# First attention: experts' down projection transposed over 512 tokens, gates spread by transfers, scores first in a chunk

## The chip, the cores and the metric

The kernel runs on one core of a Trainium2 chip. The time is that of the device for one launch, in microseconds (us); the kernel before takes 3878.38 us, the median of three runs (3876.18 to 3879.57). The core has TensorE (PE in the rows; its weight loads are PEld), VectorE (DVE), ScalarE (ACT), GpSimd (POOL) and SyncE (SP), which issues the transfers. Each runs its own list of instructions in order and waits for the others by semaphores. TensorE writes to PSUM only, which is eight banks of 128 x 512 float32.

## What is computed

16 sequences of 1024 tokens with 256 features go through two layers; all is float32. The first layer, cut to what matters:

```
xn = layernorm(x)
q, k, v = xn Wq, xn Wk, xn Wv                      # 16 heads of 16
g = log_sigmoid(xn Wgk1 Wgk2 + bgk2) / 16          # decay of each key feature
state = state * exp(g) + v k^T ; out = state q     # token by token
s = (layernorm(out) * gamma + beta) * silu(xn Wg) @ Wout
gates = softmax of the 2 largest of xn @ w_gate    # 8 experts, others 0
h = relu(xn @ Wd[e] + bd[e])                       # 8 experts of 64
f = sum over e of gates[e] * 0.5 * (h[e] @ Wu[e] + bu[e])
x = x + s * silu(f)
```

The second layer is a windowed attention with softmax and a ternary ffn of 1024 hidden features, joined in the same way.

## The kernel before

The body of the loop holds eight sequences one after another and is run twice. Of a sequence (NC = 8 chunks of 128 tokens) the parts are: queries and keys of the first attention for 512 tokens at a time (L1366 to L1383), the loop over chunks (from L1460), the second attention, and the ffn, in which the next sequence's norm, its routing logits, its decay inputs `z` and its first queries are made already.

In a chunk `c` TensorE goes in this order. `token_major(bank 0, c, w_vg)` makes values and output gate (512 columns, two steps over the 256 features, four records); two turns of the keys; `parity_scores` (L1432, the scores of 16 heads on 32-row parts of the array, into banks 3 to 6); `token_major(bank 2, c, w_down)`, the experts' down projection, tokens on the partitions; `cumulate(c + 1)` (L1384), the sums of the decays for the next chunk; then, with the masked scores, the output block: for each half of the features one product with the state (L1490) and 16 with the scores (L1495); four turns of `hg` (L1502); `output_turn(c - 1)` (L1411), the turn of the previous chunk's gated output; the state update (L1511); `output_project(c - 1)` (L1424); the up projection of four products of 256 columns (L1520) with the bias through the turned gates (L1526); and `attention_token_major(c)` (L1418), the turn of the output back to token rows.

VectorE in a chunk: values times decay (`vt`, L1160), output gate (`silu_g`, L1166), four masked scores (`causal_scores`, L1139), the gated output of the previous chunk (`y_tok`, L1105), bias add `hb` (L1175) and ReLU with the gates `hg` (L1179), state sum and state (L1187, L1191), `finish_chunk(c - 1)` (L1121 to L1129: gate product, residual, statistics), scaled output `o_tok` and its statistics (L1204 to L1209), `f_gate` (L1211), the next middle state (L1150), and `o_norm` (L1112). In chunk 7 six normalisations of the finished x (L1132) stand after `hg`. GpSimd makes the root of the variance, the two affine steps (L730, L734), `end_mask` (L765) and `parity_queries` for the next chunk (`qx`, L714). ScalarE makes tanh, the copies out of PSUM (`hgt`, L878, is that of the turned `hg`) and the three decays of a chunk (`decays`, L825 to L834), after a load of its function table at the first. At the end of the loop the normalised x is turned in eight steps (`chunk_turn`), four of them inside chunk 7's up projection, and the second attention begins with `queries_keys`. SyncE has one queue: loads of x, loads of the next sequence, stores.

The order on each engine is written out by hand as it stands in the code. The waits are counts of semaphores.

## Time and profile before

| what | value |
|---|---|
| median of three runs | 3878.38 us |
| profiled execution: own time, span | 3877.76 us, 3876.0 us |
| TensorE busy (its matmuls) | 3650.6 us, 94% |
| VectorE, ScalarE, GpSimd busy | 2777.5 us, 1962.9 us, 1082.2 us |
| GpSimd 128x512 products `qx` of the chunks (L714) | 136.4 us, 128 of them |
| VectorE `hb` (L1175), `hg` (L1179) | 86.9 us, 88.6 us |
| TensorE turns of `hg` (L1502) | 84.0 us, 512 of them |
| granted clock of TensorE | 0.996 |
| transfers | 62.3 MB, on average 16 GB/s |

A busy time of TensorE is no measure of how much is left there: records of matmuls overlap, so the distance from the start of one step to the start of the next is what a step costs. An idle time of an engine stands in brackets behind a row, with what ended it. All times in the rows below are from the start of the span; they are from the fifth sequence, and the other sequences go alike.

### The profile page before, as it was taken

How to read it: one execution, taken by the hardware profiler on the slowest of the kernel's cores; microseconds unless marked ns; L12 is line 12 of the kernel's file. 1: busy time of each engine (PE TensorE's matmuls, PEld its weight loads, DVE VectorE, ACT ScalarE, POOL GpSimd, SP SyncE). 2: the span in 40 equal slices, each digit the busy share in tenths (PEclk: the TensorE clock that was granted, in tenths of full speed). 3: DMA queues.
4: the chain of work that ended last, by engine and by line, in shares of the span. 5: the costliest groups of instructions: out<-in, count | busy, mean ns of one | idle time of the engine just before them, and what ended most of it. 6: DMA issues, size and time to landing. Idle time of an engine off the chain costs nothing. (4 is left out here: it accounts for less than half of the span.)

```text
span 3876.0 us, 73403 instructions
## 1 busy us (share of the span) xinstructions
PE 3650.6 (94%) x26748; PEld 2384.1 (62%) x26748; DVE 2777.5 (72%) x6223; ACT 1962.9 (51%) x4311; POOL 1082.2 (28%) x1313
## 2 busy tenths in 40 slices
PE   3999999999999999999989999999999999999999
PEld 2666566665666656566655666656666566665656
DVE  4767777777667767677666776777767766777767
ACT  2264562745536365373644726446274553636536
POOL 2323233231322313223122232323323232231322
PEclk9999999999999999999999999999999999999999
DMA  3000010000000000000000100001000010000000
GB/s 85 1 12 23 1 34 1 13 21 8 27 1 18 17 12 23 1 30 5 12 23 1 33 2 12 23 1 34 1 14 21 2 33 1 16 19 12 23 1 23
DMA packets 72652, 62.28 MB, mean 16 GB/s; under 512 B 18032, under 2 KB 71904, under 8 KB 72288
## 3 DMA queue, kind: packets, MB, share of 16 engines
q1 hardware_dynamic: 72288, 57.52, 4.9%
q8 instruction: 217, 3.56, 0.4%
q14 instruction: 147, 1.20, 0.1%
HBM read 40.72 MB, written 16.78 MB: 15 GB/s over the span
## 5 line engine op out<-in xcount | busy, mean ns | idle before, releaser
L786 POOL TENSOR_TENSOR qx<-qx 128x512 f32<-128x512 f32 x256 | 281.1, 1102 | 760.6 <-ACT qx L1003 760.6
L1251 DVE TENSOR_REDUCE row_max<-bank 128x4 f32<-128x512 f32 x512 | 339.2, 684 | 137.6 <-PE bank L1585 134.4
L1139 DVE TENSOR_TENSOR am<-bank,causal 128x512 f32<-128x512 f32 x512 | 317.2, 682 | 17.5 <-PE bank L1443 17.5
L1329 DVE TENSOR_TENSOR sq_lo<-qx,sq_hi 128x512 fp32r<-128x512 f32 x256 | 205.5, 803 | 155.0 <-ACT sq_hi L982 154.5
L1598 PE MATMUL bank<-ident,am 128*128 128x128 f32 x2048 | 297.1, 278 | 14.2 <-ACT qx L938 9.4
L1598 PEld LDWEIGHTS bank<-ident,am 128*128 128x128 f32 x2048 | 230.6, 141 | 92.1 <-issue 48.9
L1258 DVE TENSOR_TENSOR am<-bank,row_max 128x512 f32<-128x512 f32 x384 | 265.6, 692 | 14.6 <-PE bank L1598 1.1
L723 POOL TENSOR_SCALAR o_veps<-o_mom 128x1 f32<-128x1 f32 x128 | 28.5, 223 | 881.6 <-DVE o_mom L1209 879.3
L922 ACT ACTIVATE am<-am 128x512 f32<-128x512 f32 x384 | 261.1, 680 | 5.5 <-DVE am L1258 5.5
L1363 PE MATMUL bank<-w_down,xt 128*128 128x512 f32 x512 | 252.2, 615 | 0.0
L1520 PE MATMUL bank<-w_up,hgt 128*128 128x256 f32 x1024 | 246.2, 381 | 3.7 <-ACT hgt L878 3.7
L1363 PE MATMUL bank<-w_vg,xt 128*128 128x512 f32 x512 | 240.9, 593 | 0.0
L1693 PE MATMUL bank<-sq_hi,pj_t 128*128 128x512 f32 x512 | 213.7, 417 | 17.3 <-DVE sq_lo L1329 10.2
L825 ACT ACTIVATE decay_in<-bank 128x256 f32<-128x256 f32 x128 | 49.2, 384 | 340.8 <-PE bank L1396 340.6
L1520 PEld LDWEIGHTS bank<-w_up,hgt 128*128 128x128 f32 x1024 | 192.0, 190 | 31.5 <-ACT hgt L878 6.7
L780 POOL TENSOR_TENSOR xl<-xt,xh 128x1024 fp32r<-128x1024 f32 x32 | 75.5, 2359 | 457.1 <-DVE xh L1300 457.1
L1693 PE MATMUL bank<-sq_lo,pj_t 128*128 128x512 f32 x512 | 201.7, 394 | 0.0
L1003 ACT ACTIVATE qx<-bank,scale_fc 128x512 f32<-128x512 f32 x256 | 177.5, 693 | 43.5 <-PE bank L1681 43.5
L885 ACT ACTIVATE tanh_f<-bank 128x256 f32<-128x256 f32 x128 | 49.2, 384 | 289.6 <-PE bank L1526 289.6
L982 ACT CAST sq_hi<-qx 128x512 fp32r<-128x512 f32 x256 | 158.9, 621 | 68.4 <-PE bank L1693 37.0
L1187 DVE TENSOR_TENSOR state_sum<-bank,state_mid 128x256 f32<-128x256 f32 x112 | 47.6, 425 | 196.1 <-PE bank L1511 196.1
L714 POOL TENSOR_TENSOR qx<-qt,par_mask 128x512 f32<-128x512 f32 x128 | 136.4, 1066 | 176.6 <-ACT qt L436 138.3
(252 smaller groups left out, 8933.0 us busy)
## 6 DMA issues: line engine op xcount, KB each, us to landing
qt<-in_L_attn_x SPq DMA_DIRECT2D x136, 128.0 KB, 2.2
x<-in_L_attn_x SPq DMA_DIRECT2D x128, 128.0 KB, 2.3
out<-x SPq DMA_DIRECT2D x128, 128.0 KB, 1.7
x<-in_L_ffn_w_fc SPq DMA_DIRECT2D x1, 1024.0 KB, 5.7
attn<-in_L_ffn_w_proj SPq DMA_DIRECT2D x1, 1024.0 KB, 7.7
w_up<-in_L_ffn_Wu SPq DMA_DIRECT2D x1, 512.0 KB, 6.0
w_down<-in_L_ffn_Wd SPq DMA_DIRECT2D x2, 256.0 KB, 3.7
w_vg<-in_L_attn_Wv SPq DMA_DIRECT2D x1, 256.0 KB, 4.4
```

Source lines behind the costliest of these rows:

```text
L786: nc.gpsimd.tensor_tensor(sq[:, n % 3, :], relu[:, n % 3, :], relu[:, n % 3, :], ALU.mult)\
L922: nc.scalar.activation(pr[:, j], pr[:, j], ACT.Exp).then_inc(s["pr_ok"], 1)
L982: nc.scalar.copy(sq_hi[:, n % 3, :], sq[:, n % 3, :]).then_inc(s["sqh_ok"], 1)
L1003: nc.scalar.activation(relu[:, n % 3, :], bank[1 + n % 3][:], ACT.Relu, scale=scale_fc[:, n % MT:n % MT + 1]).then_inc(s["relu_ok"], 1)
L1139: nc.vector.tensor_tensor(am_tiles[:, :, j], bank[3 + j][:].rearrange("p (f e t) -> p f e t", f=2, e=2), causal[:].unsqueeze(1).unsqueeze( ...
L1251: nc.vector.tensor_reduce(row_max[:, j, :], scored, AX.X, ALU.max, negate=(j == 0))\
L1258: nc.vector.tensor_tensor(pr[:, j], scored, row_max[:, j, :].unsqueeze(2).broadcast_to([P, 4, P]), ALU.subtract).then_inc(s["sub_ok"], 1)
L1329: nc.vector.tensor_tensor(sq_lo[:, n % 3, :], sq[:, n % 3, :], sq_hi[:, n % 3, :].bitcast(F32), ALU.subtract)\
L1363: mm = nc.tensor.matmul(dst, xt[:, k, c * P:(c + 1) * P], w[:, k, :], start=(k == 0), stop=(k == KD - 1))
L1520: nc.tensor.matmul(bank[5][:, 0:D], hgt[:, j, :], w_up[:, j, :], start=(j == 0), stop=False)
L1598: mm = nc.tensor.transpose(bank[5 + n % 2][:, h * P:(h + 1) * P], pr[:, j, h, :], ident[:])
L1693: mm = nc.tensor.matmul(bank[5 + o][:], pj_t[:, m, o * P:(o + 1) * P], part[:, n % 3, :], start=(m == 0 and part is sq_hi), stop=(m == MT ...
```

## The change

- **Down projection.** `experts_down(i)` makes 128 of the 512 hidden features for 512 tokens, transposed: weights `w_down` as the stationary operand, `xt` as the moving one. Four groups (tokens 0 to 511, banks 0 to 3) stand before the loop between the queries and keys; the other four stand at the end of chunks 0 to 3, each into bank 5. ScalarE applies bias and ReLU (`experts_relu`) into `hidden_t`. `hb`, `hg`, `hgt` and their turns are gone.
- **Gates.** The gates stand in the turned gates once more as full float32 (32 rows further); ScalarE copies these rows, SyncE writes them to DRAM and reads each back to 64 partitions (two transfers of 512 KB for 512 tokens, into `g_wide`), and GpSimd multiplies the hidden features of a chunk with them (`hidden_gated`, 128x512, in place). The second 512 tokens' transfers wait for the product of chunk 3.
- **Order in a chunk.** The scores come first, then values, turn of keys, the up projection (into bank 2), the cumulative sums, the output block, in which both state products now stand ahead of all score products. Scores of chunks 1 to 4 wait for the last ReLU. On VectorE the values' product stands between the third and fourth masked scores.
- **End of the loop.** Two pairs of normalisations move to the ends of chunks 5 and 6 and their turns into chunk 7, in pairs. The query projection 1 moves ahead of the last output turn.
- Smaller: the gate turns stand before the last two keys; `u_nat`, `u_lo`, `w_kv2` share the space of `am`; the bias of the down projection is loaded once, not spread.

```diff
+    gate_banks = (1, 0)
+    up_banks = (2, 2, 2, 2, 2, 2, 2, 5)
# SyncE
+                    for g in range(NG):
+                        sp.wait_ge(s["gx_ok"], at("gx_ok", g + 1))
+                        sp.dma_start(gate_dram[g], gate_rows[8:8 + E, g * 512:(g + 1) * 512]).then_inc(s["gw_ok"], 16)
+                        sp.wait_ge(s["gw_ok"], at("gw_ok", 16 * (g + 1)))
+                        if g:
+                            sp.wait_ge(s["hm_ok"], at("hm_ok", 4))
+                        for e in range(2):
+                            rows = gate_dram[g].rearrange("(j e) t -> e j t", e=2)[e]
+                            sp.dma_start(g_wide[e * BN:(e + 1) * BN], rows.partition_broadcast(BN)).then_inc(s["gl_ok"], 16)
# GpSimd: hidden_gated(0) before the loop, hidden_gated(c + 1) after parity_queries(c + 1)
+                    def hidden_gated(c):
+                        g, cols = c // 4, slice(c % 4 * P, (c % 4 + 1) * P)
+                        pool.wait_ge(s["hr_ok"], at("hr_ok", 4 * (g + 1)))
+                        pool.wait_ge(s["gl_ok"], at("gl_ok", 32 * (g + 1)))
+                        nc.gpsimd.tensor_tensor(hidden_t[g][:, :, cols], hidden_t[g][:, :, cols], g_wide[:, :, cols], ALU.mult)\
+                          .then_inc(s["hm_ok"], 1)
+                        if c == NC - 3:
+                            rstd2(0, 0, 4)
# ScalarE, before decays(0)
+                    experts_relu(0)
+                    experts_relu(1)
+                    first_queries_keys(4)
+                    first_queries_keys(5)
+                    experts_relu(2)
+                    experts_relu(3)
+                    for b in range(NG):
+                        act.wait_ge(s["gtp_ok"], at("gtp_ok", b + 1))
+                        nc.scalar.copy(gate_rows[:, b * 512:(b + 1) * 512], bank[gate_banks[b]][32:64, :]).then_inc(s["gx_ok"], 1)
+                    for b in range(NG):
+                        nc.scalar.copy(gates_t[:, 4 * b:4 * b + 4, :], bank[gate_banks[b]][:].rearrange("p (c t) -> p c t", t=P))\
+                          .then_inc(s["gt_ok"], 1)
+                    first_queries_keys(6)
+                    first_queries_keys(7)
# VectorE, in a chunk
+                        for j in range(3):
                             causal_scores(c, j)
+                        dve.wait_ge(s["tg_ok"], at("tg_ok", c + 1))
+                        decayed_values(c)
+                        causal_scores(c, 3)
+                        output_gate(c)
                         if c:
                             gated_output(c - 1)
-                        nc.vector.tensor_add(hb[:], bank[2][:], bc_down[:]).then_inc(s["hb_ok"], 1)
-                        nc.vector.scalar_tensor_tensor(
-                            hg[:].rearrange("p (e b) -> p e b", e=E), hb[:].rearrange("p (e b) -> p e b", e=E), 0.0,
-                            g_all[:, c, :].unsqueeze(2).broadcast_to([P, E, BN]), ALU.max, ALU.mult)\
...
+                        if c in (NC - 3, NC - 2):
+                            dve.wait_ge(s["rs2"], at("rs2", 1))
+                            for b in range(2):
+                                normalise2(2 * (c - NC + 3) + b)
# TensorE, before the loop
+                    first_queries_keys(2)
+                    first_queries_keys(3)
+                    experts_down(0)
+                    experts_down(1)
+                    first_queries_keys(4)
+                    first_queries_keys(5)
+                    experts_down(2)
+                    experts_down(3)
+                    pe.wait_ge(s["gates_ok"], at("gates_ok", 7))
...
+                    first_queries_keys(6)
+                    first_queries_keys(7)
...
+                        elif c <= 4:
+                            pe.wait_ge(s["hr_ok"], at("hr_ok", 4 + c))
# TensorE, in a chunk
                     for c in range(NC):
+                        parity_scores(c)
...
+                            experts_up(c, 0)
+                            experts_up(c, 1)
                             cumulate(c + 1)
+                        else:
+                            pe.wait_ge(s["f1_ok"], at("f1_ok", c))
+                            pair_turn(0)
+                            pe.wait_ge(s["ktok_ok"], at("ktok_ok", c))
+                            pe.wait_ge(s["f2_ok"], at("f2_ok", c - 1))
+                            pair_turn(1)
...
-                        pe.wait_ge(s["hg_ok"], at("hg_ok", c + 1))
-                        for j in range(EB // P):
-                            mm = nc.tensor.transpose(bank[2][:, j * P:(j + 1) * P], hg[:, j * P:(j + 1) * P], ident[:])
...
+                        if c < 4:
+                            experts_down(4 + c)
+                        attention_token_major(c)
+                    experts_up(NC - 1, 1)
```

## Rows read from the trace of the kernel before

**Rows 1.** Busy time by stretch (start:end, us, busy by engine and instructions, clock, DMA).

```profile
1064.85:1127.21 62.36, 61.63 (x467) 41.18 (x465) 46.34 (x106) 17.06 (x45) 20.22 (x30) 1.00 0.01 2
...
1027.00:1262.80 235.80, 226.28 (x1667) 147.75 (x1667) 171.33 (x384) 121.75 (x269) 66.15 (x78) 1.00 0.05 15
```

**Rows 2.** Timeline of TensorE in a steady chunk: start, us, engine, line, operation.

```profile
1064.85 0.26 PEld L1422 LDWEIGHTS bank<-ident,ot 128*128 128x128 f32 x2
...
1065.08 0.30 PEld L1363 LDWEIGHTS bank<-w_vg,xt 128*128 128x128 f32 x2
...
1067.22 0.74 PEld L1443 LDWEIGHTS bank<-qx,k 32*128 32x128 f32 x16 [0.17 <-issue]
...
1068.29 0.30 PEld L1363 LDWEIGHTS bank<-w_down,xt 128*128 128x128 f32 x2 [0.33 <-issue]
...
1070.00 0.19 PEld L1395 LDWEIGHTS bank<-xh,cumulator 128*128 128x128 f32 x1 [0.55 <-issue]
...
1071.13 0.30 PEld L1490 LDWEIGHTS bank<-qt,state_mid 128*128 128x128 f32 x2 [0.34 <-DVE am L1139]
...
1071.55 0.38 PEld L1495 LDWEIGHTS bank<-am,vt 128*32 128x32 f32 x16
...
1073.12 0.42 PEld L1502 LDWEIGHTS bank<-ident,hg 128*128 128x128 f32 x4 [0.20 <-DVE hg L1179]
...
1073.74 0.20 PEld L1415 LDWEIGHTS bank<-ident,y_tok 128*128 128x128 f32 x2 [0.20 <-issue]
...
1074.64 0.51 PEld L1428 LDWEIGHTS bank<-w_out,yt 128*128 128x128 f32 x3 [0.20 <-ACT yt L841]
```

**Rows 3.** Timeline of VectorE and GpSimd in the same chunk.

```profile
1062.21 0.42 DVE L1187 TENSOR_TENSOR state_sum<-bank,state_mid 128x256 f32<-128x256 f32 x1 [1.76 <-PE bank L1511]
...
1065.39 0.42 DVE L1204 TENSOR_TENSOR o_tok<-bank,decay_out 128x256 f32<-128x256 f32 x1 [0.51 <-PE bank L1422]
...
1068.27 0.41 DVE L1166 SCALAR_TENSOR_TENSOR silu_g<-tanh_g,bank 128x256 f32<-128x256 f32 x1
...
1068.60 2.48 DVE L1139 TENSOR_TENSOR am<-bank,causal 128x512 f32<-128x512 f32 x4
...
1070.28 1.04 POOL L714 TENSOR_TENSOR qx<-qt,par_mask 128x512 f32<-128x512 f32 x1
...
1070.99 0.61 DVE L1105 TENSOR_TENSOR y_tok<-o_bet,silu_g 128x256 f32<-128x256 f32 x1
...
1074.66 0.42 DVE L1187 TENSOR_TENSOR state_sum<-bank,state_mid 128x256 f32<-128x256 f32 x1 [1.74 <-PE bank L1511]
```

**Rows 4.** Timeline, from the start of the loop over chunks to chunk 1's output block.

```profile
1036.61 1.65 POOL L738 TENSOR_TENSOR xl<-attn,xh 128x512 fp32r<-128x512 f32 x1 [7.01 <-DVE xh L1097]
...
1038.55 1.28 ACT L825 ACT_TABLE_LOAD   x1
...
1040.38 0.60 ACT L834 ACTIVATE decay_state<-bank 128x512 f32<-128x512 f32 x1
...
1058.64 0.49 PE L1490 MATMUL bank<-qt,state_mid 128*128 128x128 f32 x2
```

**Rows 5.** The page, section 5: a ReLU of 128x512 from PSUM on ScalarE.

```profile
L1003 ACT ACTIVATE qx<-bank,scale_fc 128x512 f32<-128x512 f32 x256 | 177.5, 693 | 43.5 <-PE bank L1681 43.5
```

**Rows 6.** The DMA issues: destination, source, queue, count, size, us to landing.

```profile
x<-in_L_ffn_w_fc SPq DMA_DIRECT2D x1, 1024.0 KB, 5.7
attn<-in_L_ffn_w_proj SPq DMA_DIRECT2D x1, 1024.0 KB, 7.7
...
b_q<-in_L_attn_bq SPq DMA_DIRECT2D x8, 0.1 KB, 1.6
```

**Rows 7.** Timeline of chunk 7 and the start of the second attention.

```profile
1133.47 0.49 PE L1490 MATMUL bank<-qt,state_mid 128*128 128x128 f32 x2 [1.05 <-DVE am L1139]
...
1135.00 2.02 DVE L1132 TENSOR_SCALAR xn<-x,moments,rstd 128x256 f32<-128x256 f32 x6
...
1147.34 0.41 PEld L1545 LDWEIGHTS bank<-xt,w_k2r 128*128 128x128 f32 x2
```

More of the change, by code:

```diff
@@ L850, in _ @@
                     decays(0)
-                    for b in range(2):
-                        act.wait_ge(s["gtp_ok"], at("gtp_ok", b + 1))
-                        nc.scalar.copy(gates_t[:, 4 * b:4 * b + 4, :], bank[gate_banks[b]][:].rearrange("p (c t) -> p c t", t=P))\
-                          .then_inc(s["gt_ok"], 1)
                     for c in range(NC):
@@ L1193, in _ @@
                         else:
[L1195 to L1196 removed]
+                            dve.wait_ge(s["rs2"], at("rs2", 2))
+                            for b in range(4, NC - 2):
                                 normalise2(b)
@@ L1399, in _ @@
                     cumulate(0)
-                    pe.wait_ge(s["gates_ok"], at("gates_ok", 6))
-                    for b in range(2):
-                        if b:
-                            pe.wait_ge(s["qk_ok"], at("qk_ok", 6))
-                        for j in range(4):
-                            mm = nc.tensor.transpose(bank[gate_banks[b]][:, j * P:(j + 1) * P], gates[:, 4 * b + j, :], ident[:])
-                        mm.then_inc(s["gtp_ok"], 1)
-                    token_major(bank[0][:], 0, w_vg).then_inc(s["vg_ok"], 1)
-                    token_major(bank[2][:], 0, w_down).then_inc(s["hp_ok"], 1)
                     def output_turn(c):
@@ L1490, in _ @@
                             nc.tensor.matmul(bank[7][:, half * P:(half + 1) * P], state_mid[:, half, :],
-                                             qt[:, half, c * P:(c + 1) * P], start=True, stop=False,
+                                             qt[:, half, c * P:(c + 1) * P], start=(half == 0), stop=False,
                                              skip_group_check=True)
+                        for half in range(2):
                             for e in range(2):
```

229 lines of the change are left out of this document (128 added, 101 removed).

## The prediction

> **What bounds the kernel now.** I read the busy time by stretch first, then one steady chunk of the first attention on TensorE, the same chunk on VectorE and GpSimd, then the start and the end of the loop over chunks, and last the transfers. One sequence takes 235.8 us; the first attention, from the first key projection at 1027.0, has 120 of them. In five steady chunks TensorE is busy 61.6 of 62.4 us, VectorE 46.3, GpSimd 20.2 [rows 1]. So a chunk (62.36 / 5 = 12.47 us) is bound by TensorE: its steps follow each other with little between them [rows 2]. VectorE has its longest wait ahead of the state sum, 1.7 us [rows 3]. The second attention and the ffn, the rest of the sequence, are not touched.
>
> The steps of a chunk, from the starts in [rows 2]: turn of the output to token rows 0.23, value and gate projection with the turn of the keys 2.14, scores 1.07, down projection 1.71, cumulative sums 1.13 with a 0.34 wait for VectorE (0.78 alone), output block 1.99, four turns of hg 0.62, then 0.90 to the output projection, and what is left of 12.47, 2.70, for output projection and up projection, by their records 0.76 and 1.94.
>
> **Work that goes from TensorE.** The turns of hg: 8 x 0.62 = 5.0 us in a sequence. The down projection stays as large: 8 groups of four records before and after, of 1.71 us each [rows 2]. Of the output block the two state products now stand together. In [rows 2] two such records take 0.42 where 128 columns twice need about 0.21 (a 512-column record takes 0.43, a quarter of 1.71), so about 0.2 goes at each change between 128x128 and 32-column products; one pair of changes goes, 0.39, bounded by 0 and 0.42. I take 0.39: the block is 1.60. On this the Trainium skill, "TensorEngine Tiling (Array Packing)", section "Tiling Modes", says that changing the tiling mode drains TensorE; it gives no price, and the 0.2 of the row stands.
>
> **Work that goes from VectorE, and what GpSimd gets.** hb and hg go, from y_tok to what is the state sum's wait now, which only shortens VectorE's lap. ScalarE gets eight ReLUs for eight copies of hgt, two copies of gate rows more and three turned-x copies fewer; its new cost is only where TensorE waits for it (below). GpSimd gets eight products of 128x512 in a sequence; parity's takes 1.04 and a contended one 1.65 [rows 3, 4]. GpSimd is idle for over half of a chunk, so their time is free, apart from what they block.
>
> **The start.** TensorE now does ten groups of 1.71 and eight turns (0.9, by four turns in 0.62 with a mode change in it) before the cumulative sums: 1027.0 + 18.0 = 1045.0. ScalarE copies the last keys (to 1045.7), then loads a table and makes three decays. In [rows 4] load and decays run from 1038.55 to 1040.98, 2.43 us, and hid behind gate turns, value and down projection. Now the scores come directly after the cumulative sums and wait for them: start 1048.2, a stall of 2.4. Scores and value projection and key turn end at 1051.4. Then the up projection waits for GpSimd's product, that for the gates' transfer. ScalarE has the gate rows at 1042.2 (down 3 ends at 1040.7, 0.2 latency, ReLU 0.69 [rows 5], and a copy of the same size, 0.6). The write to DRAM takes about 1.65 (nearest: a small transfer, 1.6), the spread of 1 MB 5.7 to 7.7 [rows 6], with 0.5 for the second issue: 1050.2 to 1052.2. I take 5.7, since its rows are long and the queue is empty then. The product 1.04 to 1.65: 1051.3 to 1053.9. So the stall is 0, with 2.5 as upper end. Up 1.94, cumulative sums 0.78, output block of chunk 0 at 1054.1, 1.60, state update 0.6 (of the 0.90), down projection 4 until 1058.05. On GpSimd the end mask and parity's product for chunk 1 are queued behind this product; both are short and wanted only after chunk 0's output block and at 1059. On ScalarE the gate's tanh now waits for the up projection ahead of the next decays, which start after the cumulative sums anyway.
>
> Here is a new wait: scores of chunks 1 to 4 wait for ScalarE's ReLU of the down projection issued just before (both use bank 5). Latency 0.2, ReLU 0.69 [rows 5], 0.05 back: 0.93, of which the turn of the output hides 0.23; everything of the next chunk is queued behind it on TensorE. So scores 1 start at 1059.0, and with 1.07 + 2.14 + 1.94 + 0.78 = 5.93 the output block of chunk 1 at 1064.9. Before it was at 1058.64 [rows 4]: 6.3 later, with 5.15 of down and 1.94 of up projection done earlier.
>
> **Chunks 1 to 7.** Output block to output block for 1 to 4: 1.60 + 0.90 + 0.76 + 1.71 + 0.93 + 5.93 = 11.83, against 12.47: 3 x 0.64 = 1.9 back. VectorE is ready in time there: scaled output to output block is 1065.39 to 1071.13 less the 0.33 of the gate, which now comes after the last scores = 5.41 [rows 2, 3], and it starts the scaled output 0.4 before the scores (0.54 after the turn, they 0.93), so it is ready 5.0 after the scores' start, and needed at 5.93. From chunk 5 on TensorE alone would need 9.4, but VectorE is now the bound: block to state sum 3.53 - 0.62 - 0.39 = 2.52; state sum to the next scaled output 2.67 ([rows 3] less its wait of 0.51), then 5.41: 10.6. GpSimd's new product stands right behind parity's, where y_tok wants to start, and y_tok already ends only 0.28 after parity's product ([rows 3], 0.61 us with it). That can hold output turn and state by 0.2 to 0.3: 10.8. Chunks 6 and 7 have two normalisations each in this lap, 0.7 (six in 2.02, [rows 7]): 11.5. So 1.7 + 1.0 + 1.0 = 3.7 back. At the output block of chunk 7 the new kernel is at 6.3 - 1.9 - 3.7 = 0.7 us behind.
>
> The Trainium skill, "SBUF — State Buffer", says that VectorE with two SBUF inputs and GpSimd lock each other out for a whole instruction. The y_tok row agrees. Taken to its worst it is the third rival below.
>
> **The end.** From chunk 7's output block to the key projection of the second attention 13.87 us [rows 7]. On the chain to the last y_tok go 0.62, 0.39 and about 0.3 (turns of x now stand earlier): 1.3. After it, query projection 1 (1.72) has moved ahead; in its place 0.7 of waiting for yt stays: 1.0. Together 2.3, bounds 1.0 and 2.7.
>
> **Sum.** 0.7 - 2.3 = -1.6 us in a sequence, 16 x 1.6 = 25. The profiled execution had 3877.8 (span 3876.0), 0.6 under the median: 3853. A smaller bias load and the move of small weights at the start are within 1 us; they stand behind w_down, last in the queue. SP's next entry, the next sequence's loads, comes long after the gates'. Second group of gates: asked for after the product of chunk 3, it has a whole lap of 11.8 for about 6.2, and costs nothing unless it takes twice that; GpSimd's next affine step is queued behind it.
>
> **Rivals.**
> A. The gates come late (slower): DRAM write, completion, 1 MB of reads and the product form one chain of 9.1 us that ends when TensorE arrives. It decides from 1.6 us later on; at its upper ends (7.7 and 1.65) it costs 2.5: 0.9 x 16 = +15, 3893; if the repeated read of eight rows takes 10 us, 4.3 x 16 - 25 = +44. For it: nothing hides it and the whole start waits in order. Against: a row of 1 MB at 5.7.
> B. VectorE's lap isn't the bound, because waits in it overlap more than I see: chunks 5 to 7 take 9.5 to 10.2, 3 to 4 us less in a sequence: 3800. Against it: its steps come in fixed order, and rows carry each.
> C. The lock: y_tok always waits for the whole product, also in chunks 1 to 4, and normalisations meet GpSimd: 0.75 x 3 and some more: 2 to 3 in a sequence, 3890. Against it: GpSimd's steps are over when the state's come.
> D. Gains and stalls cancel, since all terms above (2.4, 4 x 0.7, laps) are near the 8.1 that TensorE saves: within 0.2%.
>
> **How the numbers follow.** Less than 0.2% (7.8 us) can hardly be told from no change. Forecast near 3853: 0.47; A 0.2; B 0.12; C 0.08; D 0.13. Faster 0.47 + 0.12 = 0.59, same 0.13, slower 0.28. The range takes in A's first price, C and most of B: 3808 to 3900.
>
> **What would show it.** Start: a TensorE idle of 2.4 before scores 0 released by ScalarE's decay_state; the product of chunk 0 ending near 1051. Chunks 1 to 4: 11.8 apart, 0.7 idle before the scores, released by the ReLU. Chunks 5 to 7: 10.8 to 11.5, TensorE idle before the output block, VectorE hardly idle. No turns of hg; output block 1.6. Key projection of the second attention 1.6 earlier. I am wrong if the start stalls at the up projection, if chunk 5 takes over 11.5, or if the second attention and ffn change their length.

## The result and the profile after

The changed kernel is slower. Its median is 3984.18 us (3981.94 to 3988.03, four runs) beside 3877.43 us of the kernel before on the same chip (3876.18 to 3879.57, four runs): ratio 1.0276, 95% interval 1.0258 to 1.0294. The forecast was 3853, its range ended at 3900. The profiled execution took 3983.88 us, its span is 3982.1 us (before 3876.0).

The page of the changed kernel, section 1 (busy us, share of the span, instructions):

```profile
PE 3577.9 (90%) x26236; PEld 2361.6 (59%) x26236; DVE 2637.5 (66%) x5983; ACT 2003.1 (50%) x4295; POOL 1265.4 (32%) x1473
```

And the view of the core, with its span and granted clock:

```profile
core 0: 3982.1 us, clock 0.980
```

TensorE's matmuls are busy for 72.7 us less than before (3650.6) and its share fell from 94% to 90%: the work went, and idle time came that is larger. The granted clock fell from 0.996 to 0.980. The trace of the granted clock shows TensorE at the lower of its two levels (1.2 instead of 2.4 GHz) for 163 us of the launch, and for 30 us before.

Next I measured stages, by the starts of the output blocks (ob) of chunks 0 to 7, the first product of a sequence's first key projection, and `w_k2r` of the second attention. Means over 14 sequences in us (the one at the loop's turn and the last are left out); "forecast" is worked out from the prediction's steps (its 13.87 us for the end counted to the weight load of `w_k2r`; to the first product it is 14.08, so the forecast stands here as 14.08 less 2.3):

| stage | before | forecast | after | at 1.2 GHz, after |
|---|---|---|---|---|
| first key projection to ob 0 | 20.31 | 27.1 | 28.88 | 2.79 |
| ob 0 to 1 | 11.42 | 10.8 | 10.51 | 0 |
| ob 1 to 4, three laps | 37.43 | 35.5 | 37.35 | 0 |
| ob 4 to 5 | 12.47 | 10.8 | 11.17 | 0 |
| ob 5 to 6 | 12.47 | 11.5 | 12.33 | 0 |
| ob 6 to 7 | 12.47 | 11.5 | 13.06 | 2.58 |
| ob 7 to `w_k2r` | 14.08 | 11.8 | 14.18 | 4.00 |
| rest of the sequence | 115.47 | the same | 115.36 | 0 |
| sum | 236.1 | 234.5 | 242.8 | 9.4 |

So 6.7 us more in a sequence, 16 times: 107 us, the whole difference. The forecast is missed by 8.3 us in a sequence, in five places: the start (+1.8), the laps of chunks 1 to 4 (+1.9), the laps 4 to 6 (+0.4, +0.8), the lap to chunk 7 (+1.6) and the end (+2.4); the lap from 0 to 1 came out 0.3 shorter than forecast.

What TensorE waited for in the whole launch (line that waited, what it waited for, us in total, times, longest):

```profile
PE bank L1499 <- ACT ot L930: 65.2, 112, 0.6
PE bank L1592 <- DVE am L1191: 47.8, 48, 2.0
...
PE bank L1527 <- ACT attn L849: 41.7, 64, 0.7
PE bank L1527 <- ACT decay_state L881: 39.7, 16, 2.5
PE bank L1537 <- DVE xn L1184: 25.4, 16, 1.7
PE bank L1488 <- DVE am L1191: 24.1, 32, 1.4
...
PE bank L1555 <- POOL qx L769: 6.0, 6, 1.2
```

Third and fourth are the two waits of the forecast (0.65 before scores 1 to 4, 2.48 before scores 0). The first, 112 times 0.58 us, was not in it: the output turn waits for ScalarE's copy `ot`, because the turns of `hg` that stood between them are gone. TensorE before, in the chunk of [rows 2]:

```profile
1072.54 0.64 PE L1495 MATMUL bank<-am,vt 128*32 128x128 f32 x16
1073.12 0.66 PE L1502 MATMUL bank<-ident,hg 128*128 128x128 f32 x4
1073.77 0.41 PE L1415 MATMUL bank<-ident,y_tok 128*128 128x128 f32 x2
```

From the end of the output block (1073.18) to the output turn are 0.59 us here too, and the turns of `hg` fill them. Of the waits of the changed kernel, the second, fifth and sixth are VectorE's laps in chunks 5 to 7. The last is the transfer's, and it is only 6.0 us in 6 times. The kernel before waited 37 us for the masked scores in all.

TensorE's timeline of the start (fifth sequence; start us, us, line, names; the idle time before it and what ended it in brackets). It answers to [rows 4]:

```profile
1054.61 3.60 PE L1438 MATMUL bank<-xt,w_k 128*128 128x512 f32 x8
...
1076.00 1.73 PE L1527 MATMUL bank<-qx,k 32*128 32x256 f32 x16 [2.48 <-ACT decay_state L881]
1077.66 3.05 PE L1417 MATMUL bank<-w_vg,xt 128*128 128x512 f32 x4
...
1080.76 1.89 PE L1555 MATMUL bank<-w_up,qx 128*128 128x256 f32 x8
```

GpSimd in the same stretch, the product with the gates:

```profile
1078.97 1.27 POOL L769 TENSOR_TENSOR qx<-qx,g_wide 128x512 f32<-128x512 f32 x1 [7.43 <-DMA g_wide<-gate_rows]
```

Busy times by stretch of the changed kernel, one stretch behind each of three waits (us; PE, PEld, DVE, ACT, POOL; granted clock; DMA):

```profile
1076.00:1080.70 4.70, 4.70 (x22) 2.47 (x23) 2.31 (x4) 0.00 (x0) 1.73 (x2) 0.64 0.38 72
1155.00:1158.40 3.40, 2.82 (x38) 2.07 (x37) 0.65 (x1) 0.64 (x2) 0.37 (x1) 0.51 0.02 5
1168.00:1175.50 7.50, 6.81 (x48) 5.25 (x49) 1.39 (x6) 0.74 (x2) 0.00 (x0) 0.54 0.00 0
```

Behind the wait of 2.48 us the clock is 0.64 on average, and scores and value projection take 1.73 and 3.05 us instead of 1.15 and 1.98. The up projection starts at 1080.76, 0.5 us after GpSimd's product has ended (1080.24): in this sequence the late transfer is covered by a slow clock.

TensorE's timeline in chunk 2, a lap that was to be 11.83 us:

```profile
1100.61 1.15 PE L1527 MATMUL bank<-qx,k 32*128 32x256 f32 x16 [0.65 <-ACT attn L849]
1101.68 1.98 PE L1417 MATMUL bank<-w_vg,xt 128*128 128x512 f32 x4
...
1106.27 0.61 PE L1592 MATMUL bank<-qt,state_mid 128*128 128x128 f32 x4
1106.81 1.08 PE L1598 MATMUL bank<-am,vt 128*32 128x128 f32 x32
1108.47 0.41 PE L1499 MATMUL bank<-ident,y_tok 128*128 128x128 f32 x2 [0.58 <-ACT ot L930]
```

TensorE in chunks 6 and 7:

```profile
1153.14 0.35 PE L1488 MATMUL bank<-xh,cumulator 128*128 128x256 f32 x1 [1.26 <-DVE am L1191]
...
1154.58 0.92 PE L1592 MATMUL bank<-qt,state_mid 128*128 128x128 f32 x4 [0.50 <-DVE am L1191]
1155.43 1.94 PE L1598 MATMUL bank<-am,vt 128*32 128x128 f32 x32
...
1165.47 0.63 PE L1537 MATMUL bank<-ident,xn 128*128 128x128 f32 x4 [1.69 <-DVE xn L1184]
1168.10 0.81 PE L1592 MATMUL bank<-qt,state_mid 128*128 128x128 f32 x4 [2.00 <-DVE am L1191]
```

And VectorE in chunk 6, with the last pair of normalisations in chunk 7:

```profile
1150.66 1.14 DVE L1184 TENSOR_SCALAR xn<-x,moments,rstd 128x256 f32<-128x256 f32 x2
...
1154.78 0.87 DVE L1157 TENSOR_TENSOR y_tok<-o_bet,silu_g 128x256 f32<-128x256 f32 x1
...
1168.64 0.72 DVE L1184 TENSOR_SCALAR xn<-x,moments,rstd 128x256 f32<-128x256 f32 x2
```

In chunk 2 the output block is 1.62 us from its start to the end of its last product (1106.27 to 1107.89; before, counted the same way, 2.05: 1071.13 to 1073.18). The forecast's 1.60 and 1.99 of [rows 2] are counted from start to start, so they compare only roughly. The wait before the scores is 0.65 as forecast, and ahead of the output turn TensorE stands idle for 0.58. In chunk 6 TensorE waits 1.26 and 0.50 for VectorE's masked scores, in chunk 7 1.69 for the second pair of normalisations and 2.00 for the scores. Behind these waits the clock is 0.51 and 0.54: the 32 score products take 1.94 where they took 1.08. The two normalisations take 1.14 us beside GpSimd's affine step (`o_gam`, 1150.82 to 1151.65), and 0.72 at 1168.64, where no instruction of GpSimd runs; `y_tok` takes 0.87 beside the product with the gates.

### The profile page after: what moved, and what is told of

It is laid out like the page before. It is cut to its first block and busy times, and to the rows that moved or that the text cites. A ratio compares the mean times of both kernels' runs of the same rounds, so it can differ in the third digit from the quotient of the medians.

```text
span 3982.1 us, 72507 instructions
## 1 busy us (share of the span) xinstructions
PE 3577.9 (90%) x26236; PEld 2361.6 (59%) x26236; DVE 2637.5 (66%) x5983; ACT 2003.1 (50%) x4295; POOL 1265.4 (32%) x1473
## 5 line engine op out<-in xcount | busy, mean ns | idle before, releaser
L1191 DVE TENSOR_TENSOR am<-bank,causal 128x512 f32<-128x512 f32 x512 | 327.0, 679 | 14.6 <-PE bank L1527 14.6
L907 ACT ACTIVATE tanh_g<-bank 128x256 f32<-128x256 f32 x128 | 49.2, 384 | 492.9 <-PE bank L1417 492.9
L1417 PE MATMUL bank<-w_vg,xt 128*128 128x512 f32 x512 | 266.3, 645 | 0.0
L1458 PE MATMUL bank<-xt,w_down 128*128 128x512 f32 x512 | 235.4, 592 | 0.0
L1527 PE MATMUL bank<-qx,k 32*128 32x256 f32 x2048 | 151.2, 409 | 81.3 <-ACT attn L849 41.7
L989 ACT COPY xn<-bank 128x512 f32<-128x512 f32 x256 | 154.0, 608 | 55.5 <-PE bank L1690 52.4
L1768 PE MATMUL bank<-xh,fc_t 128*128 128x512 f32 x512 | 173.9, 420 | 0.0
```

The costliest lines, as they stand in the source:

```text
L1191: nc.vector.tensor_tensor(am_tiles[:, :, j], bank[3 + j][:].rearrange("p (f e t) -> p f e t", f=2, e=2), causal[:].unsqueeze(1).unsqueeze( ...
L1417: mm = nc.tensor.matmul(dst, xt[:, k, c * P:(c + 1) * P], w[:, k, :], start=(k == 0), stop=(k == KD - 1))
L1458: mm = nc.tensor.matmul(bank[5 if g else j][:], w_down[:, k, j * P:(j + 1) * P], xt[:, k, g * 512:(g + 1) * 512], start=(k == 0), stop=(k ...
L1527: mm = nc.tensor.matmul(bank[3 + j][:, half * 2 * P:(half + 1) * 2 * P], kt[rows, half, c * P:(c + 1) * P], qp[rows, c % 2, half], start=T ...
L1768: nc.tensor.matmul(h_bank, fc_t[:, k, m * P:(m + 1) * P], t[:, g, k, :], start=(t is xh and k == 0), stop=False)
```

## The experiments

All runs of one batch share the runs of the kernel before (medians 3875.4 to 3877.2). Edits are of the changed kernel if nothing else is said.

**e1, the clock: useless work in the gaps.**

```diff
                     for c in range(NC):
+                        if c == 0:
+                            fill(bank[2][:, 0:D], 5)
...
+                            fill(bank[1][:, D:2 * D], 3)
                             pair_turn(1)
+                            fill(bank[7][:, 0:D], 4)
```

`fill(dst, n)` makes `n` products of `w_out` with itself, 256 columns each, whose result nobody reads.

> The changed kernel with useless products of TensorE put where it now stands idle: 5 of 256 columns (0.43 us each) ahead of the scores of chunk 0, 3 and 4 in chunk 7 ahead of the second pair of turns and of the output block. No wait is taken away. Theory 1 (the new idle lets the granted clock fall, and the work behind it runs at half speed: 163 us at the lower level in the changed kernel against 30 before): the time at the lower level goes to below 60 us, laps 6 to 7 and the end of the loop become 0.8 and 1.9 us shorter, the start 0.3, in all some 3 us in a sequence: 3935 (3920 to 3950). Theory 2 (only the waits themselves cost; the clock is a side effect of no weight): no gain, 3984 or a little more.

Measured: 3956.34 us, ratio 1.0208 (1.0191 to 1.0225), 28 us less than the changed kernel with more work in it. Time at 1.2 GHz fell from 163 to 62 us. The end went from 14.18 to 12.57 us; the start only from 28.88 to 28.59. TensorE's timeline of the start in e1 says why:

```profile
1066.67 2.32 PE L1563 MATMUL bank<-w_out 128*128 128x256 f32 x10
1069.31 1.15 PE L1527 MATMUL bank<-qx,k 32*128 32x256 f32 x16 [0.32 <-issue]
...
1073.51 1.99 PE L1555 MATMUL bank<-w_up,qx 128*128 128x256 f32 x8 [0.92 <-POOL qx L769]
```

Scores 0 and the values run at full clock, and now TensorE is at the up projection 0.92 us before the gates. What the clock gives back in the start the transfer takes. At the end of the loop nothing stood behind. So the clock is a cause, worth at least 28 us, but not the 49 us that I had expected: the end gave 1.6 us in a sequence, the start 0.3, and in the lap to chunk 7 nothing was won (2.4 us at 1.2 GHz for 2.6, 13.07 us for 13.06), although the longest wait for the masked scores there fell from 2.0 to 0.5 us.

**e2, the waits: another order in the chunk.** State update, output turn, down projection, then the output projection:

```diff
                             mm.then_inc(s["ds_ok"], 1)
+                        if c:
+                            output_turn(c - 1)
+                        if c < 4:
+                            experts_down(4 + c)
                         if c:
                             output_project(c - 1)
-                        if c < 4:
-                            experts_down(4 + c)
```

> The changed kernel with the state update ahead of the output turn, the down projection between output turn and output projection in chunks 1 to 3, and the first half of the last up projection ahead of the output turn in chunk 7. Theory A (the output turn waits 0.58 for ScalarE's copy of the output block, which the turns of hg used to hide, and the scores wait 0.65 for the ReLU): laps 1 to 4 go from 12.45 to 11.2 each, the end of the loop is 0.6 shorter, laps 4 to 7 stay (bound by VectorE's chain through the output projection), 4.3 us in a sequence: 3984 - 69 = 3915. Theory B (these waits only move: something else is as late): laps stay near 12.4, 3975 to 3985.

Measured: 3985.12 us, 1.0281 (1.0264 to 1.0299). Both waits are gone from the three laps between chunks 1 and 4 (the ReLU's stays before scores 1, 0.65 us in 16 times), and nothing is won; the three laps took 12.12, 12.21 and 12.78 us instead of 12.45, 0.24 us less together, and the end 14.33 instead of 14.18. That is the expectation's theory B. VectorE ahead of chunk 2's masks in e2:

```profile
1100.82 0.42 DVE L1173 SCALAR_TENSOR_TENSOR sf<-f_gate,bank 128x256 f32<-128x256 f32 x1 [2.05 <-PE bank L1512]
```

TensorE in the same chunk of e2:

```profile
1106.28 0.36 PE L1488 MATMUL bank<-xh,cumulator 128*128 128x256 f32 x1 [0.22 <-DVE am L1191]
...
1107.71 0.71 PE L1592 MATMUL bank<-qt,state_mid 128*128 128x128 f32 x4 [0.49 <-DVE am L1191]
```

`sf` needs the output projection, which came later, and waits 2.05 us (0.26 in the changed kernel); so the masked scores come later, and TensorE waits for them. So VectorE's chain from the output projection to the masks was close behind TensorE. The lap to chunk 4 has one thing more, on VectorE in e2:

```profile
1125.72 1.00 DVE L1176 TENSOR_TENSOR x<-x,sf 128x256 f32<-128x256 f32 x1
```

GpSimd beside it:

```profile
1125.17 1.27 POOL L769 TENSOR_TENSOR attn<-attn,g_wide 128x512 f32<-128x512 f32 x1 [4.71 <-ACT attn L849]
```

The residual add, 0.42 us in other chunks, takes 1.00 while GpSimd multiplies chunk 4's hidden features, which wait for the last ReLU: 0.58 us, the difference between 12.78 and 12.2.

**e3 and e4, the transfer under another order.** In chunk 0 values and turn of the keys stand ahead of the scores; e4 also has no transfers, and its hidden features are multiplied by ones, so it leaves the gates out of the up projection's main part.

```diff
                     for c in range(NC):
-                        parity_scores(c)
                         if c:
+                            parity_scores(c)
...
                             mm.then_inc(s["kp_ok"], 1)
+                            if c == 0:
+                                parity_scores(0)
                             experts_up(c, 0)
```

> The changed kernel with values, output gate and turn of the keys ahead of the scores in chunk 0 alone, as before: 2.1 us of work under the wait for ScalarE's decays. Theory C (the gates' transfer stands just behind that wait: its product ends 0.5 us before TensorE comes): start to the first output block goes from 28.9 to 28.4 only, 3976. Theory D (the wait of 2.5 us and the fall of the clock after it are all that holds the start): 28.9 to 25.3, 3926.

> As the run before, and without the gates' transfers: the hidden features are multiplied by ones that are set once, so the gates are left out of the up projection's main part. Theory C: now the start goes to 25.3 (3.1 us less than with the transfers), 3926 to 3935. Theory D: the same as the run before.

Measured: e3 4006.75 us, 1.0336 (1.0315 to 1.0357), start 30.46 us; e4 3934.92 us, 1.0153 (1.0136 to 1.017), start 25.72. In e3 the values hide all but 0.54 us of the decays, and TensorE is at the up projection 22.5 us after the sequence's first key projection (1060.33) instead of 26.1. There it waits (its timeline in e3):

```profile
1081.72 1.15 PE L1527 MATMUL bank<-qx,k 32*128 32x256 f32 x16 [0.54 <-issue]
1085.98 3.68 PE L1555 MATMUL bank<-w_up,qx 128*128 128x256 f32 x8 [3.11 <-POOL qx L769]
```

3.11 us of waiting, and the up projection then takes 3.2 us until its last step instead of 1.54: what was a wait for ScalarE has become a longer wait for the transfer, with half the clock behind it. The pair gives the transfer's full price in this order, 4.7 us in a sequence. It is not its price in the changed kernel, which e8 measures.

**e5, the normalisations back at the end.** Undoes the moves to chunks 5 and 6; all six normalisations stand in chunk 7 again.

```diff
-                        if c in (NC - 3, NC - 2):
-                            dve.wait_ge(s["rs2"], at("rs2", 1))
-                            for b in range(2):
-                                normalise2(2 * (c - NC + 3) + b)
...
-                            for b in range(4, NC - 2):
+                            for b in range(NC - 2):
# TensorE: pair_turn(0) and pair_turn(1) behind attention_token_major(NC - 1)
```

> Undoes one part of the change: the six normalisations stand together in chunk 7 again and the first two pair turns stand behind the last output projection, as in the kernel before. Own theory (the move costs more in chunks 5 and 6 than it saves at the end): the steps from output block 5 to 6 and 6 to 7 fall from 12.33 and 13.06 us to about 11.2 each, as the step from 4 to 5 has it, and the stage from output block 7 to w_k2r grows from 14.18 us by 1 to 2 us, so -1 to -2 us in each of the 16 sequences: 3952 to 3968 us. Rival (the normalisations only change place, as VectorE has the same work): the end grows by the full 3.0 us, 3980 to 3990 us.

Measured: 3943.91 us, 1.0169 (1.0152 to 1.0186), 40 us less than the changed kernel, more than I had expected. The laps to chunks 6 and 7 fell to 11.28 and 11.38 us, and the end stayed at 14.07 (14.18); 0.8 of the 1.7 us won in the lap to chunk 7 goes with the time at 1.2 GHz, which fell there from 2.6 to 0.1 us. The start was 0.4 longer (29.32), with 4.5 us at 1.2 GHz instead of 2.8, in the same order of work. TensorE's output block of chunk 7 in e5:

```profile
1159.02 0.68 PE L1584 MATMUL bank<-qt,state_mid 128*128 128x128 f32 x4 [3.86 <-DVE am L1190]
```

VectorE's timeline in the same chunk:

```profile
1159.71 1.70 DVE L1183 TENSOR_SCALAR xn<-x,moments,rstd 128x256 f32<-128x256 f32 x5
1164.78 0.42 DVE L1172 SCALAR_TENSOR_TENSOR sf<-f_gate,bank 128x256 f32<-128x256 f32 x1 [3.37 <-PE bank L1507]
```

The normalisations stand where VectorE has 3.37 us of idle time behind them: there they cost nothing. Moved into laps that VectorE bounds, they cost their whole time and the clock besides.

**e6, one part of the change alone in the kernel before: the order in the output block.**

```diff
-                                             ... start=True, stop=False,
+                                             ... start=(half == 0), stop=False,
                                              skip_group_check=True)
+                        for half in range(2):
                             for e in range(2):
```

> The kernel before with one part of the change alone: in the output block the two state products stand together, ahead of the 32 products of 32 columns. It took 1.99 us per chunk before and 1.60 us in the changed kernel. Own theory (TensorE's instructions set the laps of before, and VectorE has about 1 us of slack in them): 8 times 0.39 us in each of 16 sequences, -50 us, so about 3826 us (3820 to 3835). Rival (VectorE or the copies of ScalarE are close behind and take the place): 3850 to 3876 us.

Measured: 3835.98 us, 0.9896 (0.9879 to 0.9912): faster than both kernels. A lap went from 12.47 to 12.15 us, 0.32 instead of 0.39. A wait for VectorE stands where the other 0.07 may be; its timeline in e6 has:

```profile
1060.59 0.69 DVE L1179 SCALAR_TENSOR_TENSOR hg<-hb,g_all 128x512 f32<-128x512 f32 x1
```

And TensorE in the same chunk of e6, output block and turns of `hg`:

```profile
1059.47 0.71 PE L1490 MATMUL bank<-qt,state_mid 128*128 128x128 f32 x4
...
1061.33 0.66 PE L1503 MATMUL bank<-ident,hg 128*128 128x128 f32 x4
```

`hg` ends at 1061.28 and its turns start at 1061.33, 0.13 after the output block (1061.20). From its start to that end the block takes 1.73 instead of 2.05, which is the 0.32. What the block would give without `hg` behind it was not measured.

**e7, cover for the copy `ot`.** The cumulative sums of the next chunk stand behind the output block; ScalarE makes the decays behind `ot` and `yt`.

```diff
                             experts_up(c, 1)
-                            cumulate(c + 1)
...
                         mm.then_inc(s["ot_ok"], 1)
+                        if c + 1 < NC:
+                            cumulate(c + 1)
                         if c:
                             output_turn(c - 1)
```

> The changed kernel with the 0.70 us of the next chunk's cumulated decays on TensorE moved from ahead of the output block to right behind it, and ScalarE's three decay activations behind its copies ot and yt. Own theory (the hidden activations' turns of before covered 0.58 us in which TensorE now waits for ScalarE's copy ot before the output's turns): the steps from output block 1 to 4 fall from 12.45 us to about 11.87, so 3 times 0.58 us in 16 sequences, -28 us, with up to 15 us more from the chunks behind: 3940 to 3957 us. Rival (the wait only moves, to the decays' products or to VectorE): 3975 to 3990 us.

Measured: 3958.3 us, 1.0216 (1.0199 to 1.0233), 26 us less than the changed kernel. The laps from 1 to 2 and 2 to 3 are 11.89 and 11.88 us (12.45), the forecast's 11.83 but for 0.05. The third, from 3 to 4, is 12.36: TensorE waits 0.32 us for the masks in chunk 4, since VectorE's `state_mid` ran beside GpSimd's product for chunk 4 (0.77 us for 0.42) and GpSimd's root for `o_norm` stands behind that product. TensorE's timeline of e7 in chunks 3 and 4:

```profile
1110.94 0.39 PE L1489 MATMUL bank<-xh,cumulator 128*128 128x256 f32 x1
...
1111.75 0.38 PE L1500 MATMUL bank<-ident,y_tok 128*128 128x128 f32 x2
...
1121.75 0.71 PE L1592 MATMUL bank<-qt,state_mid 128*128 128x128 f32 x4 [0.32 <-DVE am L1192]
```

VectorE in chunk 4's lap of e7:

```profile
1117.02 0.77 DVE L1203 TENSOR_TENSOR state_mid<-state,decay_state 128x256 f32<-128x256 f32 x1
```

The turn at 1111.75 has no idle time before it. So the 0.58 is ScalarE's copy, uncovered by the removal of the turns of `hg`. Of the 26 us about 20 come from these three laps. The start is 0.8 us shorter (28.08), because the sums for chunk 1 stand behind its output block now, and the laps 4 to 5 and 5 to 6 are 0.2 and 0.1 longer: from chunk 4 on the wait for the copy is gone and a longer one for the masked scores stands there (107 us for `am` in the launch instead of 72). Chunk 7, where no sums are left to move, keeps its 0.58.

**e8, the changed kernel without the transfers, and e12, the same with e1's useless products.** The diff of both takes out SyncE's loop over `g` and GpSimd's wait on `gl_ok`, and sets `g_wide` to ones; both leave the gates out of the up projection's main part.

> The changed kernel without the transfers that write the gate rows out and spread them over the partitions; the hidden activations are multiplied by ones, so the gates are left out of the down path. Order of the work as in the changed kernel. Own theory (with the scores first the transfer has 7 us of cover, and TensorE reaches the up projection at most 0.6 us after the product is there): the start to output block 0 goes from 28.88 to 28.0 to 28.9 us, total 3970 to 3984 us. Rival (the transfer is on the path as in the run with the values' product first, where taking it away gave 4.7 us in each sequence): start about 24.2 us, total about 3910 us.

> The first fill run (useless products ahead of scores 0, in chunk 7 and behind it) without the transfers that spread the gates; the hidden activations are multiplied by ones, so the gates are left out of the down path. In the changed kernel taking the transfers away gave nothing, but the one sequence without half clock in its start took 27.06 us there against 28.3 with the transfers. Theory (half clock and transfer hide each other, each worth 1 to 1.3 us): with the clock held, start to output block 0 falls from 28.25 to 27.1 us, total 3935 to 3942 us. Rival (the transfer costs nothing in either case): 3953 to 3960 us.

Measured: e8 3986.65 us, 1.0279 (1.0262 to 1.0296), no gain. e12 3928.91 us, 1.0132 (1.0116 to 1.0149), 27 us less than e1. Starts of single sequences tell it best, us:

| start of a sequence | with the transfers | without |
|---|---|---|
| part of it at 1.2 GHz, the most frequent value (changed kernel, e8) | 28.7 | 28.7 |
| none at 1.2 GHz (changed kernel five times, e8 once) | 28.2 to 28.5 | 27.06 |
| with useless products, none at 1.2 GHz (e1, e12) | 28.1 to 28.4 | 27.06 |

The two prices hide each other: 1.2 us of late gates and up to 1.6 us of half clock, and the start pays the larger. Either one taken away alone gives nearly nothing (e1: 0.3 us, e8: none). With both away it takes the 27.1 us of the forecast. Between the profiled spans of e1 and e12 are 30 us. The start gives 1.25 x 16 = 20, by the means 28.59 and 27.34; the rest lies in the lap to chunk 7, where the clock held in e12 (12.28 us for 13.07) and not in e1, with the same order of work in it. So of the 27 us between e1 and e12 only these 20 are the transfer's price.

**e9, a start without the wait.** On TensorE the four down projections follow keys 2 and 3, then the turns of the gates, queries and keys 4 and 5, the cumulative sums, 6 and 7.

```diff
                     experts_down(1)
-                    first_queries_keys(4)
-                    first_queries_keys(5)
                     experts_down(2)
                     experts_down(3)
... the turns of the gates
+                    first_queries_keys(4)
+                    first_queries_keys(5)
+                    cumulate(0)
                     first_queries_keys(6)
                     first_queries_keys(7)
-                    cumulate(0)
# ScalarE: gate rows ahead of ReLU 2 and 3, decays(0) ahead of the copies of 6 and 7
```

> The changed kernel with another order ahead of scores 0, on TensorE: keys 2 and 3, the four down projections, the gates' turns, keys and queries 4 and 5, the cumulated decays of chunk 0, then 6 and 7 (before: the cumulated decays last). ScalarE copies the gate rows ahead of ReLU 2 and 3, and makes the decays ahead of the copies of 6 and 7. Own theory (the 2.48 us in which scores 0 wait for decay_state, and the half granted clock that follows it, are what the start took beyond its work): no wait before scores 0, so start to output block 0 from 28.88 us to 24.7 to 26.7, total 3920 to 3950 us. Rival (the transfer of the gates or ScalarE ends last instead): start 27.5 to 28.9 us, total 3960 to 3984 us.

Measured: 3928.97 us, 1.0135 (1.0118 to 1.0152), 55 us less than the changed kernel, as expected. The start takes 25.61 us on average, 25.33 in most sequences. TensorE's timeline of the start in e9:

```profile
1055.84 3.60 PE L1438 MATMUL bank<-xt,w_k 128*128 128x512 f32 x8
1059.37 1.15 PE L1527 MATMUL bank<-qx,k 32*128 32x256 f32 x16
...
1062.48 1.91 PE L1555 MATMUL bank<-w_up,qx 128*128 128x256 f32 x8
```

The gates' product on GpSimd in e9:

```profile
1061.07 1.27 POOL L769 TENSOR_TENSOR qx<-qx,g_wide 128x512 f32<-128x512 f32 x1 [4.44 <-DMA g_wide<-gate_rows]
```

No idle time before scores 0, full clock, and the product of the gates ends at 1062.34, 0.14 us before it is wanted. The wait for the decays was a matter of the order: the load of the function table and the decays (2.4 us) have two projections of 1.7 us to hide behind, if the sums stand before them.

**e10 and e11, the repairs together.** e10 has the edits of e5, e7 and e9, and in chunk 7 the up projection ahead of the output block, where e5 waits 3.86 us; e11 adds three useless products there.

> Four edits of the changed kernel together: the start's order of e9; the cumulated decays behind the output block; the normalisations and pair turns back in chunk 7; and in chunk 7 the whole up projection (1.9 us) ahead of the output block, where TensorE waited 3.86 us for VectorE's masks. If the parts add up: 3984 - 40 (norms at the end) - 26 (cumulated decays) - 34 to 62 (start) - 15 to 30 (up projection) = 3826 to 3869 us. If they share one bound, VectorE's lap of 11.3 to 11.9 us: 3870 to 3900 us.

> e10 with three useless products of 128 x 256 (0.43 us each) in chunk 7 ahead of the output block, inside the wait for VectorE's masks. Clock theory (the half granted clock behind that wait costs 1.3 to 1.5 us in each sequence): 20 us faster than e10 if the clock still falls there. Rival (with the up projection in that place the wait is too short for the clock to fall): the same as e10 within 5 us.

Measured: e10 3852.28 us, 0.9939 (0.9922 to 0.9955); e11 3840.3 us, 0.9905 (0.9888 to 0.9921). TensorE at the output block of chunk 7 in e10:

```profile
1122.76 0.71 PE L1583 MATMUL bank<-qt,state_mid 128*128 128x128 f32 x4 [1.76 <-DVE am L1189]
```

e11, the useless products and the output block:

```profile
1121.78 1.46 PE L1557 MATMUL bank<-w_out 128*128 128x256 f32 x6
1123.70 0.71 PE L1590 MATMUL bank<-qt,state_mid 128*128 128x128 f32 x4 [0.47 <-DVE am L1189]
```

With 1.76 us of waiting at this place e10 still spends 2.93 us of an end at 1.2 GHz on average: none in the first eight sequences, some in seven of the last eight, with the same wait in all. With 0.47 e11 spends none, the end takes 12.43 us in every sequence (13.36 on average in e10), and the launch is 12 us shorter. The parts add up: 55.2 + 40.3 + 25.9 = 121.4 us for e9, e5 and e7 singly; e10 has 10.5 more, which is put down to its up projection but was not run alone; e11 12.0 more; together 143.9, from 3984.2 to 3840.3.

## Why the prediction was wrong, point by point

**The sum.** Of the 8.3 us missed in a sequence, 4.1 are the wait for ScalarE's copy `ot` (seven chunks of 0.58), which the prediction put at nothing; 2.4 are the half clock in the end (1.6, e1) and in the lap to chunk 7 (0.8, by the sequences without it); 1.8 are the start, where late gates and half clock hide each other; 0.9 are the two pairs of normalisations (0.46 each over the 0.7 forecast). Against them stand 0.6 that I had added for GpSimd in the laps 4 to 7 and 0.3 in the lap 0 to 1. These terms add up to 8.3 and were worked out one by one from the laps; repairs that take them away singly give less, since the next wait is close (e2, e7).

**The bound.** Right: before, TensorE's own instructions set a chunk. Removing 0.32 us of them gave 41 us (e6).

**What goes from TensorE.** The output block is 1.62 us, forecast 1.60. In the changed kernel its gain is in the laps as taken. The turns of `hg` are gone too, 0.62 us a chunk, but here the first step fails. The prediction booked 0.62 in full and "0.90 to the output projection" behind it as fixed. The turns had been cover for the way from the output block over ScalarE's copy to the output turn, and without them 0.58 us of waiting stands there in every chunk but the first: 65.2 us in the launch. I had asked of every wait I added what it blocks, and not of the work I removed what it hid. Before, the same 0.59 us were there, filled by the turns, so that their removal gave almost nothing. e7 shows the cover by putting 0.70 us of other work in their place.

**The start.** Three steps. The wait of 2.4 us for the decays came out as said (2.48). The chain of the gates was mis-sized: row copy to end of the product is 1069.86 to 1080.24, 10.4 us, where I had 9.1 (the terms written there add up to 8.9). The nearest row, one load of 1 MB in 5.7 us, with 0.5 for the second issue, was too short for the two reads: from the first one's issue at 1071.34 the product waits 7.6 us. The write took 1.5 where I had 1.65, the product 1.27 where I had 1.04. That is rival A within its bounds, 1.3 of its 2.5 us, and e12 against e1 gives 1.2. The third step is missing: behind 2.48 us of idle time the granted clock was half. Transfer and clock hide each other (e8), so that the start came out 1.8 us too long and not 3. Where both are away (e12) it takes 27.06 us in most sequences, the 27.1 of the forecast.

**Chunks 1 to 4.** 35.5 forecast, 37.35 measured; two of the three laps came to 11.89 and 11.88 in e7, where the forecast had 11.83 each. The new wait for the ReLU is as forecast (0.65 for 0.68 to 0.70), the wait for `ot` is the error. VectorE was ready in time, as said, but only just: e2 shows that a later output projection makes it the bound at once.

**Chunks 5 to 7.** That VectorE would be the bound is right. Lap 4 to 5 is 10.6 + 0.58 = 11.18 by my chain with the missed wait in it, measured 11.17; what I had added for GpSimd, 0.2, was not there. The pairs of normalisations were taken at 0.7 and cost 1.16 (12.33 - 11.17), since they run beside GpSimd's affine step; e5, which takes them out, gives 1.05 (12.33 - 11.28). That is rival C in another place than I had put it. On this the Trainium skill, "SBUF — State Buffer", says that GpSimd and a VectorE instruction that has two SBUF inputs, or runs in a mode with two ports, lock each other out of a shared pair of ports for a whole instruction. The rows agree for two inputs: the residual add of e2 took 1.00 and `state_mid` of e7 0.77 instead of 0.42. Two normalisations, which have one large input each, took 1.14 beside `o_gam` and 0.72 without it; in which mode they ran no row shows.

**The end.** 11.8 forecast, 14.18 measured. I had taken 2.3 us off for work gone and moved, and counted the moved normalisations only where they went, not asking whether they had cost anything where they were. e5 says that they had cost nothing: the end is 14.07 with them. And the end runs 4.0 us at half clock; with the clock held it takes 12.4 to 12.6 (e1, e11). The 0.8 that is left in e1 is the wait for `ot` in chunk 7 (0.58) and 0.2 that were not followed up.

**The clock.** No step of the prediction and no rival had it. The trace of before had the sign, 30 us at the lower level in the whole launch and no wait of TensorE over 1.3 us in the loop over chunks. The changed kernel has one of 2.48 in the start, and a pair of 1.69 and 2.00 in chunk 7. The Trainium skill, "TensorE: Matmul & The Clock Gate", Part 1, says that a hardware block watches how busy TensorE is and gates its clock between the two levels. The traces agree in kind: low stretches stand behind the new idle time and nowhere in the steady laps, 163 us in the changed kernel and 37 in e11, where the first two of these waits are gone and the third is 0.47. A wait of this length did not bring the lower level each time: 2.48 us stand before scores 0 in all sequences of the changed kernel, and in five of the 14 the start has none of it. A removed wait saved more than itself here: e9 won 55 us, where 16 waits of 2.48 are 40, but the rest is not the clock's alone, since e9 also has the gates in time.

**Together.** The forecast's gains on TensorE were real as work (72.7 us less busy), and all of them and more were turned into waits: 65 us for `ot`, 97 us for VectorE's scores and normalisations (before, 37 for the scores), 42 for the ReLU, 40 for the decays. What stays open is why the clock fell in some sequences and not in others of the same kernel: in the lap to chunk 7 (2.4 us a sequence in e1, none in e12), in the start, and in e10's last eight ends. And the wait for the ReLU was only removed by moving the down projection ahead of the output projection (e2); a version that covers it otherwise was not made.

## What to carry to other kernels

Before booking removed work as a gain, look at what is issued right behind it and what that waits for: the removed work may be the cover of a round trip through another engine. A part that moves work into an idle place should be checked from both ends, and work that stands in an engine's idle time, like the normalisations here (e5), may cost nothing where it is. Try the parts of a large change one by one: here the smallest, the order of two products, was worth 41 us alone (3836 us), and everything else in the change, even repaired (3840 us), brought nothing that can be told from it.

## What was not expected of the hardware

- TensorE's granted clock fell to half behind waits of some 2 us in a stream that is otherwise busy (0.51 to 0.64 in the stretches above), though not behind each of them, and 32 score products then took 1.94 us for 1.08. Useless products in the gap shortened the launch by 28 us (e1) and 12 us (e11).
- Two delays in one place did not add: late gates (1.2 us) and half clock (up to 1.6 us) each cost nothing while the other was there.
- A write of 16 KB to DRAM and two reads of 512 KB from it, each repeating the same rows for 64 partitions, took 1.5 us and 7.6 us to the product's start. The DMA rows have a median of 6.7 us to landing for one of the reads over the launch.
